# Two-layer post-norm decoder on one core: rounding of the feed-forward on GpSimd, query blocks placed anew, first pass reordered

## The reference, cut to what matters

```
x = norm(x + attn0(x))            # 16 heads of 64, softmax(q k^T / 64) v, times WO
x = norm(x + xattn0(x, ctx))      # 16 heads of 16
x = norm(x + ffn0(x))             # see below
x = norm(x + attn1(x))            # decay attention with gates, then squared leaky relu MLP 256 -> 768 -> 256
x = norm(x + xattn1(x, ctx))      # two key sets, softmax over the queries
x = norm(x + coupled_ffn(x))      # three cycles of a small gelu network

def _act_quant(x):                # one scale for each token
    scale = 127.0 / clip(max(abs(x), axis=-1), 1e-05)
    return clip(round(x * scale), -128, 127) / scale
ffn0(x) = q(silu(q(x) @ Wg) * (q(x) @ Wu)) @ Wd    # q = _act_quant, weights in three levels, 256 -> 1024 -> 256
```

## Time and profile before

| what | value |
|---|---|
| time, median of 3 runs | 1188.82 us (1186.34 to 1189.29) |
| time of the profiled execution | 1191.58 us |
| its span, first to last instruction | 1189.4 us |
| mean granted TensorE clock over the span | 0.984 |
| TensorE matmul busy | 1060.7 us, 89% |
| VectorE busy | 772.1 us, 65% |
| ScalarE busy | 652.4 us, 55% |
| GpSimd busy | 322.7 us, 27% |

### The profile page before, as it was taken

One profiled execution on the slowest core, in us unless ns is written; L12 is line 12 of the kernel. 1 busy time (PEld: TensorE's weight loads), 2 busy tenths in 40 slices (PEclk: granted clock), 3 DMA queues, 4 the chain that ended last, 5 costly groups with the idle time before them and its releaser, 6 DMA issues.

```text
span 1189.4 us, 19960 instructions
## 1 busy us (share of the span) xinstructions
PE 1060.7 (89%) x7313; PEld 691.1 (58%) x7313; DVE 772.1 (65%) x1866; ACT 652.4 (55%) x1744; POOL 322.7 (27%) x670
## 2 busy tenths in 40 slices
PE   7899888999899988899899999899989997789985
PEld 3466544775656744675566654477565564477552
DVE  0764478557778468565857657755867837955776
ACT  2475256348478455546658734635847835434843
POOL 1154301131136410232025630113014641023111
PEclk9999899999999999998999999999999999999998
DMA  9630000000000000000000000000000000000000
GB/s 274 175 94 1 18 1 9 1 1 1 1 18 2 19 19 1 9 1 1 2 1 19 19 18 2 9 1 1 2 1 1 20 1 2 1 1 1 2 1 18
DMA packets 30496, 22.79 MB, mean 19 GB/s; under 512 B 16704, under 2 KB 29504, under 8 KB 30272
## 3 DMA queue, kind: packets, MB, share of 16 engines
q1 hardware_dynamic: 29952, 21.50, 6.6%
q10 hardware_dynamic: 448, 0.02, 0.0%
HBM read 19.42 MB, written 2.10 MB: 18 GB/s over the span
## 4 chain that ended last, share of the span: by engine, by line
PE 59%; DVE 20%; ACT 10%; issue 6%; POOL 4%; DMA 0%; SPq 0%; POOLq 0%; DVEq 0%; ACTq 0%
PE PS L554 7%; PE PS L719 5%; PE PS L541 4%; PE PS L964 4%; PE PS L705 3%; PE PS L591 3%; ACT work L1533 3%; PE PS L807 3%; PE PS L688 3%; PE PS L670 2%; POOL work L2262 2%; PE PS L938 2%; PE PS L977 2%; ACT work L1348 2%; DVE work L1844 2%
## 5 line engine op out<-in xcount | busy, mean ns | idle before, releaser
L2234 POOL TENSOR_TENSOR rstd<-var,minus_half 128x2 f32<-128x2 f32 x64 | 46.2, 722 | 436.6 <-DVE var L1661 436.2
L1533 ACT ACTIVATE work<-PS,nmax 120x256 f32<-120x256 f32 x256 | 118.1, 485 | 25.6 <-DVE nmax L2072 24.6
L2262 POOL TENSOR_SCALAR work<-work,inv 128x256 f32<-128x256 f32 x256 | 119.7, 487 | 0.0
L1348 ACT ACTIVATE work<-PS,nmax 128x256 f32<-128x256 f32 x256 | 118.3, 483 | 1.1 <-DVE nmax L1720 1.1
L2072 DVE TENSOR_REDUCE nmax<-PS 120x2 f32<-120x512 f32 x128 | 82.7, 685 | 44.2 <-PE PS L964 43.9
L1720 DVE TENSOR_REDUCE nmax<-PS 128x2 f32<-128x512 f32 x128 | 82.2, 684 | 20.0 <-PE PS L670 19.8
L2229 POOL TENSOR_TENSOR pool_pause<-minus_half 128x1 f32<-128x1 f32 x96 | 30.3, 315 | 227.5 <-DVE inv L1727 116.0
L964 PE MATMUL PS<-x_room 32*120 32x256 f32 x512 | 68.7, 401 | 12.7 <-ACT work L1533 8.8
L670 PE MATMUL PS<-work 64*128 64x256 f32 x512 | 74.2, 401 | 1.9 <-ACT work L1348 1.9
L705 PE MATMUL PS<-work 128*64 128x256 f32 x512 | 70.3, 396 | 1.5 <-DVE work L1740 1.1
L964 PEld LDWEIGHTS PS<-x_room 32*120 32x120 f32 x512 | 42.1, 178 | 40.5 <-issue 33.0
(11 more groups left out here) (280 smaller groups left out, 2441.2 us busy)
## 6 DMA issues: line engine op xcount, KB each, us to landing
turned_x<-in_xT_dram SPq DMA_DIRECT2D x8, 256.0 KB, 3.0
xa<-in_x_dram SPq DMA_DIRECT2D x4, 512.0 KB, 3.9
rows<-in_rows_dram SPq DMA_DIRECT2D x1, 1536.0 KB, 13.5
late<-in_L_attn_W_dram SPq DMA_DIRECT2D x2, 768.0 KB, 7.9
out_dram<-x_room SPq DMA_DIRECT2D x3, 512.0 KB, 3.4
wv<-in_L_attn_kernel_dram SPq DMA_DIRECT2D x4, 256.0 KB, 5.1
wq<-in_L_attn_kernel_dram SPq DMA_DIRECT2D x2, 512.0 KB, 7.2
wk<-in_L_attn_kernel_dram SPq DMA_DIRECT2D x2, 512.0 KB, 7.6
```

Source lines behind the costliest of these rows:

```text
L1348: op = act.activation(e0[:, u % 2, st, hh, :], bank(2 * (u % 2) + hh)[:, st * S:(st + 1) * S], ACT.Exp, bias=nmax0[:, u % 2, hh, st:st + 1 ...
L1533: op = act.activation(e1[:, par, r, kv, :], bank(SCORE_1[r])[0:M, kv * S:(kv + 1) * S], ACT.Exp, bias=nmax1[:, par, r, kv:kv + 1], accum_o ...
L2262: op = pool.tensor_scalar(e0[:, u % 2, st, hh, :], e0[:, u % 2, st, hh, :], inv0[:, u % 2, hh, st:st + 1], 1.0, ALU.mult, ALU.mult)
```

## The change

- ffn0, VectorE: clip and division by 127 become one operation (`qstep`, `hstep`), and the inverse of that is the scale itself, so one small operation of each chain goes. The rounding of the second half of the input (two tiles) and of hidden tiles 0 to 2 is no longer in VectorE's program; VectorE rounds hidden tile 3 alone, behind a wait for the rounding of tile 2.
- ffn0, GpSimd: `quantize_second` and `round_hidden(it, 0..2)` stand behind `rstds_of(it, "2")` in its program.
- TensorE, passes 0 to 2: query block 4 moves from between the two `turn_sum3` to behind `decays`, block 5 from there to behind the first `turn_normed` "m"; `turn_sum3(it, 1)` moves ahead of `gates(it, 0)`; blocks 6 and 7 are computed in halves of one sequence each, around `queries_1(it, 0)` and around `scores_1(it, 4)`. ScalarE's copies move with them.
- TensorE, pass 3: products that nobody reads are placed anew, 4 to 2, 4, 4; 3 to 3 and 4; 7 to 4 and 3.
- Pass 0: key blocks 6 and 7 leave `project_first` and stand in units 0 and 1 of `attn0`, as in the other passes. `fold_norm(3)` moves behind the first norm of `cross0`.

The diff, cut; left out are the new names of two small tiles and lines of context:

```diff
@@ -362,14 +362,14 @@
-        a_max, a_clip, a_inv, a_scales, a_scale, a_tmp, a_q = signal_rounds(
-            "a_steps", ("max", "clip", "inverse", "later scales", "scale", "rounding", "quantized"), TS)
+        a_max, a_step, a_inv, a_scales = signal_rounds("a_steps", ("max", "step", "inverse", "later scales"), TS)
+        a_tmp, a_q = signal_rounds("a_quantized", ("rounding", "quantized"), TS)
...
-        h_max, h_clip, h_inv, h_down, h_scale, h_tmp = signal_rounds(
-            "h_steps", ("max", "clip", "inverse", "later scale", "scale", "rounding"), T)
+        h_max, h_step, h_inv, h_down = signal_rounds("h_steps", ("max", "step", "inverse", "later scale"), T)
+        h_tmp = signal("h_tmp", T)
@@ -592,6 +592,16 @@
+            def half_queries0(it, j, b):
+
+                if b == 0:
+                    pe.wait_ge(q0_kept.sem, q0_kept.at(it, j))
+                for k in range(KD):
+                    mm = pe.matmul(bank(7)[:, b * S:(b + 1) * S], wq0[:, k, j * P:(j + 1) * P],
+                                   turned_x[:, k, b * S:(b + 1) * S], start=(k == 0), stop=(k == KD - 1))
+                if b == NB - 1:
+                    mm.then_inc(q0_done.sem, 1)
+
@@ -601,6 +611,8 @@
+                    elif j == 6 and first_pass(it):
+                        pe.wait_ge(k0_kept.sem, k0_kept.at(it, j - 1))
@@ -643,7 +655,7 @@
                 total_weights()
-                for j in range(J):
+                for j in range(J - 2):
@@ -1096,10 +1108,11 @@
                         scores0(it, u + 1, last)
-                    if last is not None and u == 0:
+                    if u == 0:
                         both_keys0(it, J - 2)
-                        turn_final(last, 1)
-                    if last is not None and u == 1:
+                        if last is not None:
+                            turn_final(last, 1)
+                    if u == 1:
                         both_keys0(it, J - 1)
@@ -1203,26 +1216,28 @@
                 turn_sum3(it, 0)
+                if then is None:
+                    idle_products(2)
+                turn_sum3(it, 1)
                 gates(it, 0)
                 values_m(it, 0)
-                if then is not None:
-                    queries0(then, 4)
-                else:
-                    idle_products(4)
-                turn_sum3(it, 1)
                 gates(it, 1)
                 outputs_m(it, 0)
                 values_m(it, 1)
                 outputs_m(it, 1)
                 decays(it)
                 if then is not None:
-                    queries0(then, 5)
+                    queries0(then, 4)
                 else:
                     idle_products(4)
                 attend_m(it)
                 for kv in range(2):
                     context1_values(it, kv)
                 turn_normed(it, "m", xs["m"], 0)
+                if then is not None:
+                    queries0(then, 5)
+                else:
+                    idle_products(4)
@@ -1234,10 +1249,14 @@
                 if then is not None:
-                    queries0(then, 6)
+                    half_queries0(then, 6, 0)
                 else:
                     idle_products(3)
                 queries_1(it, 0)
+                if then is not None:
+                    half_queries0(then, 6, 1)
+                else:
+                    idle_products(4)
                 for n in range(0, GX * HC, 2):
                     scores_1(it, n)
@@ -1247,9 +1266,14 @@
                         turn_normed(it, "x4", xs["4"], 1)
                         if then is not None:
-                            queries0(then, 7)
+                            half_queries0(then, 7, 0)
                         else:
-                            idle_products(7)
+                            idle_products(4)
+                    if n == 4:
+                        if then is not None:
+                            half_queries0(then, 7, 1)
+                        else:
+                            idle_products(3)
@@ -1367,7 +1391,7 @@
-                    if last is not None and u in (0, 1):
+                    if u in (0, 1):
                         keep_k0(it, J - 2 + u)
@@ -1465,8 +1489,6 @@
                 keep(it, "h", 0)
-                if then is not None:
-                    keep_q0(then, 4)
                 keep(it, "h", 1)
@@ -1486,8 +1508,10 @@
                 if then is not None:
+                    keep_q0(then, 4)
+                keep(it, "m", 0, col["L1_attn_ln2_g"], col["L1_attn_ln2_b"])
+                if then is not None:
                     keep_q0(then, 5)
-                keep(it, "m", 0, col["L1_attn_ln2_g"], col["L1_attn_ln2_b"])
@@ -1512,14 +1536,14 @@
                 keep(it, "x4", 0)
+                keep_queries(it, 0, QUERY_1[0], q1, col["L1_xattn_bq"], q1_done, q1_kept)
                 if then is not None:
                     keep_q0(then, 6)
-                keep_queries(it, 0, QUERY_1[0], q1, col["L1_xattn_bq"], q1_done, q1_kept)
...
-                        if then is not None:
-                            keep_q0(then, 7)
+                    if n == 6 and then is not None:
+                        keep_q0(then, 7)
@@ -1784,9 +1808,6 @@
                 dve.wait_ge(x_in.sem, x_in.at(it, 16))
-                if first_pass(it):
-                    fold_norm(3)
-
                 def sum_1(b):
@@ -1794,6 +1815,8 @@
                 sum_1(0)
                 norm_summed(it, "1", 0)
                 apply_norm(it, "1", of(res), xs["1"], 0)
+                if first_pass(it):
+                    fold_norm(3)
                 sum_1(1)
@@ -1809,15 +1832,14 @@
-                    dve.tensor_scalar(amax[:, h], amax[:, h], 1e-5, None, ALU.max).then_inc(a_clip.sem, 1)
-                    dve.wait_ge(a_clip.sem, a_clip.at(it, hf + 1))
-                    dve.reciprocal(qinv[:, h], amax[:, h]).then_inc(a_inv.sem, 1)
-                    dve.tensor_scalar(gate_scale[:, h], amax[:, h], w_mean[:, 0:1], 1.0 / 127, ALU.mult, ALU.mult)
-                    dve.tensor_scalar(up_scale[:, h], amax[:, h], w_mean[:, 1:2], 1.0 / 127, ALU.mult, ALU.mult
-                                      ).then_inc(a_scales.sem, 1)
+                    dve.tensor_scalar(qstep[:, h], amax[:, h], 1e-5, 1.0 / 127, ALU.max, ALU.mult).then_inc(a_step.sem, 1)
+                    dve.wait_ge(a_step.sem, a_step.at(it, hf + 1))
+                    dve.reciprocal(qscale[:, h], qstep[:, h]).then_inc(a_inv.sem, 1)
+                    dve.tensor_scalar(gate_scale[:, h], qstep[:, h], w_mean[:, 0:1], None, ALU.mult)
+                    dve.tensor_scalar(up_scale[:, h], qstep[:, h], w_mean[:, 1:2], None, ALU.mult).then_inc(a_scales.sem, 1)
+                    if hf > 0:
+                        return
                     dve.wait_ge(a_inv.sem, a_inv.at(it, hf + 1))
-                    dve.tensor_scalar(qscale[:, h], qinv[:, h], 127.0, None, ALU.mult).then_inc(a_scale.sem, 1)
-                    dve.wait_ge(a_scale.sem, a_scale.at(it, hf + 1))
                     for t in (2 * hf, 2 * hf + 1):
@@ -1871,16 +1893,15 @@
-                    dve.tensor_scalar(hmax[:, one], hmax[:, one], 1e-5, None, ALU.max).then_inc(h_clip.sem, 1)
-                    dve.wait_ge(h_clip.sem, h_clip.at(it, t + 1))
-                    dve.reciprocal(hinv[:, one], hmax[:, one]).then_inc(h_inv.sem, 1)
-                    dve.tensor_scalar(down_scale[:, one], hmax[:, one], w_mean[:, 2:3], 1.0 / 127, ALU.mult, ALU.mult
-                                      ).then_inc(h_down.sem, 1)
-                    dve.wait_ge(h_inv.sem, h_inv.at(it, t + 1))
-                    dve.tensor_scalar(hscale[:, one], hinv[:, one], 127.0, None, ALU.mult).then_inc(h_scale.sem, 1)
-                    dve.wait_ge(h_scale.sem, h_scale.at(it, t + 1))
-                    dve.tensor_scalar(hid[:, t % 2, :], hid[:, t % 2, :], hscale[:, one], MAGIC, ALU.mult, ALU.add
-                                      ).then_inc(h_tmp.sem, 1)
+                    dve.tensor_scalar(hstep[:, one], hmax[:, one], 1e-5, 1.0 / 127, ALU.max, ALU.mult).then_inc(h_step.sem, 1)
+                    dve.wait_ge(h_step.sem, h_step.at(it, t + 1))
+                    dve.reciprocal(hscale[:, one], hstep[:, one]).then_inc(h_inv.sem, 1)
+                    dve.tensor_scalar(down_scale[:, one], hstep[:, one], w_mean[:, 2:3], None, ALU.mult).then_inc(h_down.sem, 1)
+                    if t == T - 1:
+                        dve.wait_ge(h_inv.sem, h_inv.at(it, T))
+                        dve.wait_ge(h_tmp.sem, h_tmp.at(it, T - 1))
+                        dve.tensor_scalar(hid[:, t % 2, :], hid[:, t % 2, :], hscale[:, one], MAGIC, ALU.mult, ALU.add
+                                          ).then_inc(h_tmp.sem, 1)
@@ -2251,6 +2272,22 @@
+            def quantize_second(it):
+                pool.wait_ge(a_inv.sem, a_inv.at(it, TS))
+                pool.wait_ge(normed["2"].sem, normed["2"].at(it, NB))
+                pause(0)
```

(15 more changed lines are left out.)

4 lines of the change are left out of this document (2 added, 2 removed).

## The result

The changed kernel took **1163.09 us** in the median of 4 runs (1158.54 to 1165.76), the kernel before beside it 1189.05 us: a ratio of 0.978 (95% interval 0.976 to 0.980). Forecast were 1159.5 us and 1153 to 1171. The profiled execution took 1161.76 us, its span is 1160.0 us.

A forecast was written before the change was run, and what follows sets the result against it. TensorE, busy 89% of the span, was taken as the bound: its work plus its waits. Terms 12.75 + 2.7 + 4.5 + 6.1 + 3.2 = 29.3 us off 1191.6 gave 1162.3, less 2.8 for the median 1159.5; range 1153 to 1171.

The forecast's parts named there:

- opening and cross0 of pass 0: Pass 0: moved key blocks and `fold_norm(3)` fill TensorE's waits and end low clock there: 4.5 and 6.1 us less.
- ffn0, a pass of three: ffn0, passes 0 to 2: shorter VectorE chain, rounding on GpSimd, second product and `up(2)` earlier: 0.75 us less a pass.
- attn1, a pass of three: attn1, passes 0 to 2: moved query blocks cover TensorE's waits for ScalarE's copies: 2.7 us less a pass.
- cross1, a pass of three: cross1, passes 0 to 2: half blocks fill the wait for copied queries, scores begin earlier: 0.8 us less a pass.
- pass 3, ffn0 and attn1: Pass 3: 1.1 us in ffn0, 1.3 us of waits in attn1 and fewer unread products: 2.7 us less.
- low clock in cross1: cross1, all passes: falls of the clock lose 6.5 us, of which half was taken as gain: 3.2 us.
- The price on GpSimd: ffn0: rounding 1024 columns on GpSimd taken as 1.16 us, from rows of multiplications by a scalar.
- The slack: ffn0: hidden tile 1 rounded on GpSimd at 473.8 against 474.0 before, so nothing lost.
- The slower rival: ffn0: GpSimd's rounding as slow as 4.9 us or more, kernel slower from 5.1 us on: 1211 us, chance 0.03.
- The clock doesn't recover: Falls stay in cross1 and two occur in new places of pass 0: 21.4 us gained, 1167.4 us, chance 0.20.
- All falls go: No falls of the clock remain: 32.5 us gained, 1156.3 us, chance 0.15.
- ffn0 gives nothing: ffn0: ScalarE's queue and rounding at 1.95 us keep the chain as long: 3.3 us less gain, 1162.8 us, chance 0.10.

The follow-up runs named there:

- 5: Kernel before with only key blocks 6 and 7 moved from the opening to units 0 and 1 of pass 0: 1184.44 us, ratio 0.997.
- 6: Kernel before with only `fold_norm(3)` moved behind the first norm of cross0 in pass 0: 1183.36 us, ratio 0.996.
- 3: Changed kernel with attn1 of TensorE and ScalarE back in the old order: 1172.58 us.
- run 2: Kernel before with only the merged small operations, all rounding on VectorE: 1185.27 us, ratio 0.998.
- run 1: Changed kernel with all rounding of ffn0 back on VectorE: 1163.03 us, ratio to before 0.979.
- run 7: Changed kernel with GpSimd going over hidden tiles 0 to 2 twice (times 1.0 plus 0.0, then the rounding): 1166.65 us.
- run 8: Changed kernel with GpSimd rounding hidden tiles 0 to 2 by subtracting minus MAGIC, both scalars by pointer: 1176.49 us.
- the filled kernel: Changed kernel with unread products in the wait ahead of heads 4 of cross1 in all passes: 1158.21 us, ratio to before 0.975.
- run 4: Changed kernel with cross1 back in the old order, blocks 6 and 7 whole: 1162.10 us.
- 12: Changed kernel unaltered, run again beside the filled kernel on the same chip: 1161.05 us.

## Why the prediction was right, and where it was not

**The terms.** The spans differ by 29.4 us (1189.4 less 1160.0), the profiled executions by 29.8; the sum was 29.3. By its parts:

| term | forecast | measured, profiled executions |
|---|---|---|
| opening and cross0 of pass 0 | 10.6 | 10.6 |
| ffn0, a pass of three | 0.75 | 0.76 |
| attn1, a pass of three | 2.7 | 2.94 |
| cross1, a pass of three | 0.8 | 0.5 |
| pass 3, ffn0 and attn1 | 2.7 | 3.7 |
| low clock in cross1 | 3.2 | 3.2 |
| end of the span | none | -0.7 |

With three passes: 10.6 + 3 x 4.2 + 3.7 + 3.2 - 0.7 = 29.4. The first pass and attn1 are shown by undoing or doing them alone (5, 6, 3). Of the signs named ahead, the rounding (1.12 us), the first maximum without idleness, `down` (1.10 us) and the clock of pass 0 came as said; the copy that was L1304's still costs 0.3 us, not 0.2, and the products are 4.44 us apart, not 4.3.

**ffn0: the right size for a reason only partly right.** I led the gain from the first product starting 1.3 us earlier, for which the rounding had to leave VectorE, and then cut it to 0.75 because TensorE is the bound from there. With that cut I should have asked how little would reach it. The merged operations take 0.16 us out of the input chain twice and out of each tile's once, and run 2 shows that they alone bring 0.62 of the 0.76; GpSimd brings 0.14 (run 1). What I credited to the engine that was relieved came from the chain that was shortened. In pass 3 it is the other way: GpSimd's part is 1.3 us, the merged operations' 0.4, and I had counted 1.1 for both.

**The price on GpSimd** was forecast as 1.16 us from two rows of multiplications by a scalar, and is 1.12. The slack was read nearly right: the prediction had 0.2 us, and run 7 speaks for about 0.4. The slower rival had the wrong shape. It took four operations in a row, less 14.7 us of room for which it gave no row, so that a microsecond of price costs four and nothing is lost below 3.7 us (at 3.78 us, 0.4 a pass). Run 7 loses 0.6 us a pass at 2.17 us a tile, and run 8 loses 2.55 at 3.78 us at full clock. The onset is earlier and the slope gentler, about 1.2 us for a microsecond between those two; that even this form stays faster than before (1176.5 us) agrees with the rival's break even at 5.1.

**The miss of 3.6 us against the median** lies in the clock. The profiled execution of before was among the slowest of its runs because it had more low clock than the others: its mean clock is 0.984, and beside the runs of experiment 1 before took 1186.2 us at 0.990, 1188.5 at 0.987 and 1191.7 at 0.984. I took off 2.8 us for that and, in the term of the clock in cross1, 3.2 us of the same falls: they were counted twice. With all falls of the earlier trace rows gone the sum ends at 1191.6 - 32.5 = 1159.1, and that is where runs without them lie (1158.2 filled, 1158.5 for the changed kernel's fastest, at clock 0.995); the forecast of 1159.5 meant to leave half of them in, and left 0.4 us. Without the 2.8 us the sum gives 1162.3, and the measured medians are 1163.1 and 1161.05.

The term itself holds for the two profiled executions and hardly for the medians. The other terms add up to 26.2 us (10.6 + 3 x 4.2 + 3.7 - 0.7), and the medians differ by 26.0 (1189.05 less 1163.09) and 27.9 (1188.94 less 1161.05), so that the clock in cross1 gave between nothing and 1.7 us. That 3.2 was forecast and 3.2 measured is luck: half was the middle of two bounds, not the outcome of a mechanism.

**The rivals.** "The clock doesn't recover" is excluded by 5 and 6 for the first pass; in cross1 half of it stayed in the profiled execution. "All falls go" (1156.3) is what the filled kernel shows, at 1158.2; its number has the 2.8 us taken off twice as well. "ffn0 gives nothing" did not come: the rounding took 1.12 us, not 1.95, and the stage gave 0.76 us a pass. For GpSimd's part of it, 0.14 us in passes 1 and 2, it is nearly right.

**What stays open.** (a) What made falls in cross1 so frequent before. In the profiled executions of before and of runs 2, 5 and 6, with both attn1 and cross1 in the old order, 12 of 16 passes fell; with one of the two in the old order (3, 4), 2 of 8; with both new and unfilled (changed, 12, 1, 7), 5 of 16. The waits around heads 0 to 6 are the same in run 4 as before; whether something ahead of them counts too, or chance made the difference, isn't shown. In time the orders differ less than in counts: ten of the twelve falls of the old order cost 1.6 us each, those of the new order 3.2 to 3.3, which makes 1.4 us a pass against 1.0. (b) The end: SyncE's last wait, for the output to land, first in the changed kernel, then in run 1:

```profile
SPq L70 <- DMA out_dram<-x_room: 2.5, 1, 2.5
```

```profile
SPq L70 <- DMA out_dram<-x_room: 1.8, 1, 1.8
```

From VectorE's last instruction to the end of the span are 2.55 us in all five kernels without GpSimd's rounding and 3.25 to 3.6 us in all nine with it. SyncE's last wait is 1.8 us in the five and 2.5 to 2.8 in the nine. Why the same output takes 0.7 to 1.0 us longer to land there isn't known, and in the changed kernel it takes back 0.7 of the 1.9 us that GpSimd's part gives.

## What to carry to other kernels

When a gain is cut off by the next bound, ask at once which is the smallest edit that reaches the cut: here one small operation less in each chain did most of what a transfer to another engine was credited with. A profiled execution with more low clock than its fellows may be corrected to the median or have its falls counted as gains, not both. And a wait of little over 1 us that costs nothing by itself may be worth filling with unread products, where what follows it is dense work for TensorE; whether it is, only the runs tell.

## What the runs showed of the hardware

- For this rounding the form of the operation on GpSimd matters more than the engine: 128 by 1024 takes 0.75 us on VectorE, and on GpSimd 1.12 us with multiply and add but 3.71 us with multiply and subtract, or 3.77 us where the second scalar is a pointer too. Columns beyond the first 256 cost 0.84 ns each in the first form ((1122 - 479) / 768). For the subtraction with two pointers it is about 3.3 ns ((3773 - 1223) / 768), an estimate, since the row of 256 columns subtracts first and multiplies then.
- The Trainium skill (GPSIMD Engine Reference, Elementwise — side-by-side cycle accounting) gives about 1.8 cycles an element at 1.2 GHz as the best case of an unrolled loop, 1.5 ns; the measured 0.84 ns is below that, so the measurement decides. The same section of the Trainium skill (GPSIMD Engine Reference, Elementwise — side-by-side cycle accounting) has 1.03 cycles an element where the read and write ports limit the loop, 0.86 ns, and the measured figure is near that one.
- VectorE's product and maximum kept their 1.28 and 1.22 us, and GpSimd its 1.12 us, while they ran beside each other (run 7); in run 8, too, where a rounding of 3.78 us lay over whole products and maxima. These forms show no sign of contention.
- A fall of the clock can follow a wait of 1.35 us in one pass and not in another of the same program, so two executions of one kernel differ by up to 3.3 us for each. With the waits filled, four runs lay within 0.32 us.
